# Graph-network layers on one core: mask stores issued by GpSimd, and the last x block normed by VectorE

## The chip, the core and the metric

The kernel runs on one core of a Trainium2 chip. The metric is device time in microseconds (us) of one launch, the median of several runs; lower is better. The core's engines are TensorE (PE), VectorE (DVE), ScalarE (ACT), GpSimd (POOL) and SyncE (SP). SP here only issues DMAs; ACT and POOL issue some too. Each of the three has a DMA queue of its own in the profile: q1 for SP, q10 for ACT, q0 for POOL.

## The reference, cut to what matters

`x` is 8192 x 128, `adj` is 8192 x 8192 float32 and holds ones and zeros.

```python
h = jnp.maximum(_layernorm(x), 0.0)
Wh = h @ W                                   # layer 0: attention over the graph
e = leaky_relu(Wh @ a1 + (Wh @ a2).T, 0.2)
att = softmax(where(adj > 0, e, -9e15), axis=-1)
x = x + relu(att @ Wh)
h = jnp.maximum(_layernorm(x), 0.0)
node = h @ W1                                # layer 1: K = 16 heads
hw = einsum('nc,kcf->nkf', h, W2)
y = adj @ einsum('nk,nkf->nf', node, hw) + node @ b
x = x + relu(y)
```

So `adj` (256 MB) is needed twice: as a mask in layer 0, and as a matrix in layer 1.

## The kernel before

**Setup.** The eight blocks of x (1024 rows each) are loaded, normed, turned by PE, passed through relu by ACT and multiplied by W and the two attention vectors. In `norm` (L1000 to L1007 for VectorE, L450 to L459 for GpSimd) VectorE norms four of a block's eight tiles and GpSimd the other four. `turn_x(i, g)` on PE (L812) transposes half g of block i and waits for VectorE (g = 0) or GpSimd (g = 1). `take_wh` on ACT copies the products out to `wh_mask`. The last step, i = 7, is x block 0. Extremes of the second attention vector then go through VectorE and PE to `gmm`, from which exponentials `bcol`, `qcol`, `zcol` and the row `zb` are made. Row z of all blocks is stored to HBM (`zrow_d`) and comes back block by block through `load_z` on GpSimd.

**Stage 1, the attention.** There are 8 blocks of 1024 output rows, and 8 half-turns to a block. One turn is two half-turns, p = 0 and 1, numbered n from 0 to 63. For a turn, four quarters c of `adj` (2 MB each, in four quadrants of 32 partitions; SP loads quadrants 0 and 1, ACT 2 and 3) come into `adj_sb`. They are cast to bytes `m8` (half h of each quarter for half-turn p = h; mostly by ACT, L612) and transposed in 32 x 32 squares by VectorE (`turn_squares`, L1020) into `mt[:, p]`, the mask tile of a half-turn. A quarter is loaded again once both of its casts are done. VectorE then weighs: eight `scalar_tensor_tensor` per half-turn (L1104) make `p_sb` from `zb`, `qcol` and the mask, and PE multiplies them (L901, 128 products of 128 x 129 per half-turn) into three PSUM banks. `squared` counts the squares, four to a half-turn.

**The mask store.** Layer 1 needs the same masks, so each `mt[:, p]`, 1 MB, is stored to `maskT_d` in HBM. This is done by ACT in `turn` (L712), at k = 0 of each half-turn, after waiting for the four squares of that half-turn: L723 to L728. VectorE waits for `mt_stored` before it writes the same buffer again, two half-turns later.

**The finish.** From block 1 on the rows of the block before are finished, one tile of 128 rows (number m) per half-turn, in `finish_tile` of each engine. VectorE divides, adds x (L1085, which waits for `kept`), takes statistics and norms (L1097). PE transposes (L879), multiplies with W1 (L867) and W2 (L872). ACT scales 16 heads into `prod` (L686). GpSimd first waits in `confirm` (L475 to L479) until the stores of the tile before have landed and counts `kept`. It then adds the heads up in `fold` (L485, L488), cuts the sum in two parts (L500, L502), stores it to `msg_d` (L505), and stores x1 and the bias to `keep_d` (L510). The last block's tiles are finished in stage 2.

**Stage 2.** The masks are read back from `maskT_d`, widened, and PE multiplies them with the messages (L960).

**Order on GpSimd.** After setup: wait for `z_stored`, `start_block(0)` (issues `load_z(1)`), then for each block from 1 on `start_block` and eight times `finish_tile`.

Of the kernel before, what the change touches and what calls it, by code (L numbers as in the profile page):

```python
# [35 lines left out]
EDGE = 64.0  # L36


def build(nc, x, adj, W, a1, a2, W1, W2, b, out):
# [34 lines left out]
    with ctx:  # L74
# [273 lines left out]
        def _(sp):  # L348

            sp.sem_inc(xt_in, 16 * A)  # L350
            load_x(sp, 1, (0, 1))
            for i in range(2, NB, 2):
                load_x_pair(sp, i, (0, 1))
# [78 lines left out]
        def _(pool):  # L432
# [30 lines left out]
            pool.tensor_scalar(f1rep, ones[:, :], wa[:, 0:1], None, ALU.mult).then_inc(f1rep_done, 1)  # L463
            for i in range(1, NB):
                norm(i)
# [50 lines left out]

            pool.wait_ge(z_stored, 16)

            def start_block(ib, last):
                if not last:  # L520
# [3 lines left out]
                    load_z(ib + 1)  # L524

            def finish_block(ib):
                with pool.Fori(0, IT) as jg:
                    for p in range(2):
                        u = ib * IT + jg
                        finish_tile(p, u, 2 * u + p)  # L530

            start_block(0, False)
            with pool.Fori(0, NB - 2) as before:
# [31 lines left out]
        def _(act):  # L565
            load_x(act, 1, (2, 3))
            for i in range(2, 6, 2):
                load_x_pair(act, i, (2, 3))
            act.sem_inc(node_copied, 1)
# [6 lines left out]
            load_x(act, 0, (2, 3))  # L576
            load_quadrants(act, 0, 0, 0, (2, 3))

# [36 lines left out]
            deviation(0)  # L615
            load_quadrants(act, 0, 0, 1, (2, 3))
            act.wait_ge(setup_pe, 1)
# [6 lines left out]
            for i in range(NB):  # L624
# [5 lines left out]
                if i < 2:  # L630
                    load_quadrants(act, 0, 0, 2 + i, (2, 3))
            act.wait_ge(setup_pe, 3)
            act.activation(w1T, mt_ps[1][0:K, 0:D], ACT.Copy).then_inc(setup_act, 1)
            cast(3, 0, 1, 0)
            act.activation(std[:, :], eps[:, :], ACT.Exp)
            act.wait_ge(setup_dve, 12)
# [9 lines left out]
            for c in range(A):  # L646
                if c >= 2:
                    cast(c, 1, 1, 0)
                if c < 3:
                    load_upper(1, c)  # L650
# [61 lines left out]
            def turn(i, ib, jg, finish, last):  # L712
                for p in range(2):
                    n = 2 * i + p
                    ends = ends_block(jg) and p == 1
                    sums_wait = ends and not finish
                    for k in range(C):

                        if k == 1:
                            load_upper(i + 1 + p, 3 - 2 * p)  # L720
                        if k == 3 and not sums_wait:
                            load_upper(i + 2, 2 * p)
                        if k == 0:  # L723
                            act.wait_ge(squared, A * n + A)
                            act.dma_start(maskT_d[bass.ds(2 * jg + p, 1), bass.ds(ib, 1), :, :]
                                          .rearrange("s i p w -> (s i p) w"),
                                          mt[:, p, :, :].rearrange("p c n -> p (c n)")).then_inc(mt_stored[p], 16)
                        if ends and last and k == 2:  # L728
                            load_xt(act, ib)
                        if ends and k == 3:  # L730
                            if last:
                                convert(0, True, 0)
                            copy_sums(ib)
                            if sums_wait:
                                load_upper(i + 2, 2 * p)
                        ahead = None if last else lambda: cast(2 * p + 1, 0, i + 2, 2 * A * i + 2 * p + 2)
                        if finish:
                            u = i - IT
                            finish_tile(k, p, u, 2 * u + p, 2 * jg + p, ib - 1, ahead)
                        elif k == 2 and ahead:  # L740
                            ahead()
                        if k < 2 and not last:
                            cast(2 * p, k, i + 2, A * (2 * i + k) + 2 * p + 1)
                        if k == (3 if sums_wait else 2) and not last:
                            cast(2 * p + 1, 1, i + 2, A * (2 * i + 1) + 2 * p + 2)
# [49 lines left out]
        def _(pe):  # L795
# [16 lines left out]
            def turn_x(i, g):  # L812
                pe.wait_ge(xn8_pool if g else xn8_done, i + 1)
                if i:
                    pe.wait_ge(hT_done, 2 * (i - 1) + g + 1)
                for j in range(4):
                    ins = pe.transpose(mt_ps[g][:, j * D:(j + 1) * D], xn8[:, i % 2, 4 * g + j, :], ident[:, :])
                ins.then_inc(xnT_done, 1)
# [16 lines left out]
            for i in range(NB):  # L835
# [3 lines left out]
                project(i)  # L839
                if i < NB - 1:  # L840
                    idle_run(4, h_ps)
            pe.wait_ge(f1rep_done, 1)
            for g in range(2):
                pe.matmul(hw_ps[g][:, :], f1rep, hT4[:, (NB - 1) % 2, g, :], start=True, stop=True).then_inc(f1_done, 1)

            pe.wait_ge(hT_done, 2 * NB)
            pe.wait_ge(par1_in, 32)
            pe.transpose(mt_ps[1][0:K, 0:D], wcat[:, K * D:K * D + K], ident[:, :]).then_inc(setup_pe, 1)
            pe.wait_ge(setup_dve, 4)
# [4 lines left out]
              .then_inc(setup_pe, 1)  # L854
            pe.wait_ge(setup_act, 3)
            pe.matmul(mt_ps[1][:, 2 * D:3 * D], hrep[:, :], w_sb[:, :], start=True, stop=True).then_inc(setup_pe, 1)
# [126 lines left out]
        def _(dve):  # L983
# [3 lines left out]
            def statistics(i):  # L987
                bk = block_of(i)
                dve.wait_ge(x_in[bk if bk < 2 else bk // 2 * 2], 16 * A)
                for n in range(T * i, T * (i + 1)):  # L990
# [7 lines left out]
            def norm(i):  # L998
# [3 lines left out]
                if i >= 2:  # L1002
                    dve.wait_ge(xnT_done, 2 * (i - 1))
                for t in range(HT):
                    n = T * i + t
                    ins = dve.tensor_scalar(xn8[:, i % 2, t, :], rows_of(block_of(i))[:, t, :], mv8[:, n, 0:1], rstd8[:, n:n + 1],
                                            ALU.subtract, ALU.mult)  # L1007
                ins.then_inc(xn8_done, 1)

# [15 lines left out]

            def first_cast(c, h):
                dve.wait_ge(adj_in[c], 16 * A)
                dve.tensor_scalar(m8[:, h, c, :].rearrange("p (t n) -> p t n", n=COLS), adj_halves[:, c, :, h, :],
                                  EDGE, None, ALU.mult).then_inc(adj_cast[h][c], 1)

            for c in range(3):
                first_cast(c, 0)
                first_squares(c)
                if c < 2:
                    first_cast(c, 1)
            dve.wait_ge(wh_copied, 3 * NB)
# [204 lines left out]
```

## Time and profile before

| | us |
|---|---|
| median of three runs | 1737.59 |
| lowest and highest run | 1735.99, 1738.54 |
| the profiled execution, whole | 1738.18 |
| its span (first to last instruction) | 1736.20 |
| PE busy | 1691.8 |
| DVE busy | 1312.7 |
| ACT busy | 1084.3 |
| POOL busy | 683.9 |

The span is 1.98 us shorter than the execution. Stage 1 runs from about 59 to 1215 us. In the chain of work that ended last PE has 66%, DMA 10%, POOL 9% and DVE 7%. "Idle before" in a row of the timeline is how long that engine had nothing to do before the row, with the releaser behind it. POOLq and ACTq are the engines' sequencers, which issue DMAs and count semaphores. The granted clock of TensorE is 0.99 of full speed over the span.

### The profile page before, as it was taken

The numbers are of one execution on the slowest core, as the hardware profiler recorded it, in microseconds if no ns is written. First come the engines' busy times: TensorE is split into PE (matmuls) and PEld (weight loads), VectorE is DVE, ScalarE is ACT, GpSimd is POOL, SyncE is SP. The second block draws the span as 40 slices with busy tenths as digits, with TensorE's granted clock in tenths as the row PEclk, the third lists the DMA queues.
The fourth block names the chain that finished last, engine by engine and source line by source line (L and its number), as shares of the span: only waits on it lengthen the run. The fifth ranks groups of instructions, "written<-read, shape, count | busy, mean of one in ns | idle before, by whom it ended". The sixth has DMA issues, their size and how long they took to land.

```text
span 1736.2 us, 34518 instructions
## 1 busy us (share of the span) xinstructions
PE 1691.8 (97%) x11272; PEld 1462.3 (84%) x11272; DVE 1312.7 (76%) x1746; ACT 1084.3 (62%) x1884; POOL 683.9 (39%) x562
## 2 busy tenths in 40 slices
PE   7899999999999999999999999999999999999997
PEld 5799988889888898898888888888677788888886
DVE  7798889989889898898899998997556443433534
ACT  4555676666766676766766767663565655555554
POOL 7000256556556565565564564655535100000000
PEclk9999999999999999999999999999999999999999
DMA  9999999999999999999999999968543345354430
GB/s 293 256 385 368 359 303 301 312 309 307 304 298 316 301 303 323 296 302 327 287 311 317 296 314 303 308 193 307 204 165 127 124 169 194 138 203 147 167 145 24
DMA packets 170639, 451.65 MB, mean 260 GB/s; under 512 B 13424, under 2 KB 13520, under 8 KB 152800
## 3 DMA queue, kind: packets, MB, share of 16 engines
q1 hardware_dynamic: 82272, 223.37, 41.2%
q10 hardware_dynamic: 81328, 208.20, 38.7%
q0 software_dynamic: 6992, 19.49, 3.4%
q8 instruction: 25, 0.41, 0.1%
q14 instruction: 22, 0.18, 0.0%
HBM read 363.94 MB, written 87.07 MB: 260 GB/s over the span
## 4 chain that ended last, share of the span: by engine, by line
PE 66%; DMA 10%; POOL 9%; DVE 7%; issue 5%; ACT 1%; ACTq 0%; POOLq 0%; DVEq 0%
PE ot_ps L901 29%; PE ot_ps L960 13%; PE mt_ps L960 13%; PE hw_ps L872 9%; DMA keep_d<-keep 6%; POOL prod L485 6%; DVE p_sb L1104 3%; DMA maskT_d<-mt 3%; DMA adj_sb<-in_adj_dram 1%; POOL msg L488 1%; DVE mt L1020 1%; ACT prod L686 1%; POOL p_sb L457 1%; POOL msg L500 1%; PE h_ps L867 1%
## 5 line engine op out<-in xcount | busy, mean ns | idle before, releaser
L901 PEld LDWEIGHTS ot_ps<-wh_mask,p_sb 128*128 128x128 f32 x8192 | 942.2, 192 | 75.4 <-issue 68.5
L901 PE MATMUL ot_ps<-wh_mask,p_sb 128*128 (+1 forms) x8192 | 951.4, 276 | 15.4 <-DVE p_sb L1104 15.4
L1104 DVE SCALAR_TENSOR_TENSOR p_sb<-zb,qcol,mt 128x1024 f32<-128x1024 uint8 (+1 forms) x512 | 740.2, 1461 | 22.4 <-DVE mt L1020 9.9
L485 POOL TENSOR_TENSOR prod<-prod 128x1024 f32<-128x1024 f32 (+2 forms) x192 | 395.0, 2057 | 460.3 <-ACT prod L686 362.2
L612 ACT ACTIVATE wh_mask<-adj_sb 128x2048 uint8<-128x2048 f32 x251 | 477.9, 1935 | 59.5 <-DMA adj_sb<-in_adj_dram 39.7
L1151 DVE CAST mask<-adj_sb 128x1024 fp32r<-128x1024 uint8 x272 | 203.8, 755 | 244.4 <-PE mt_ps L960 241.6
L709 ACT ACTIVATE mask<-adj_sb 128x1024 fp32r<-128x1024 uint8 x240 | 255.1, 1064 | 176.8 <-PE ot_ps L960 176.6
L686 ACT ACTIVATE prod<-hw_ps,node 128x128 f32<-128x128 f32 x1024 | 278.7, 383 | 114.3 <-PE hw_ps L872 113.3
L960 PE MATMUL mt_ps<-mask,msgs 128*128 128x512 f32 x1024 | 283.4, 399 | 3.9 <-DVE mask L1151 3.0
L960 PE MATMUL ot_ps<-mask,msgs 128*128 128x512 f32 x1024 | 275.5, 391 | 1.3 <-DVE mask L1151 0.9
L872 PE MATMUL hw_ps<-wcat,hT 128*128 128x512 f32 x512 | 240.7, 592 | 0.0
L960 PEld LDWEIGHTS mt_ps<-mask,msgs 128*128 128x128 f32 x1024 | 191.6, 188 | 53.3 <-issue 14.8
L960 PEld LDWEIGHTS ot_ps<-mask,msgs 128*128 128x128 f32 x1024 | 192.3, 188 | 44.1 <-issue 3.7
L1020 DVE STREAM_TRANSPOSE mt<-wh_mask 128x512 f32<-128x512 f32 x256 | 179.7, 702 | 20.1 <-DMA maskT_d<-mt 18.5
L872 PEld LDWEIGHTS hw_ps<-wcat,hT 128*128 128x128 f32 x512 | 88.6, 190 | 61.8 <-issue 61.2
L662 ACT ACTIVATE hT<-h_ps 128x128 f32<-128x128 f32 x64 | 17.8, 278 | 130.2 <-PE h_ps L879 129.9
L1085 DVE TENSOR_TENSOR keep<-att,xt 128x128 f32<-128x128 f32 x64 | 29.1, 454 | 84.8 <-POOLq L479 72.5
L488 POOL TENSOR_TENSOR msg<-prod 128x128 f32<-128x128 f32 x64 | 87.1, 1360 | 5.0
L676 ACT ACTIVATE node<-h_ps 128x16 f32<-128x16 f32 x64 | 11.8, 184 | 104.7 <-PE h_ps L867 104.7
L1097 DVE TENSOR_SCALAR xn<-keep,mv,rstd 128x128 f32<-128x128 f32 x64 | 60.6, 947 | 2.3
L513 POOL DMA_DIRECT2D zb<-zrow_d x7 | 3.9, 554 | 126.7 <-DVE p_sb L1104 101.0
L505 POOL DMA_DIRECT2D msg_d<-msg x56 | 31.8, 567 | 43.6 <-ACT keep L678 28.2
(129 smaller groups left out, 586.2 us busy)
## 6 DMA issues: line engine op xcount, KB each, us to landing
adj_sb<-in_adj_dram ACTq DMA_DIRECT2D x256, 512.0 KB, 12.2
adj_sb<-in_adj_dram SPq DMA_DIRECT2D x256, 512.0 KB, 11.0
maskT_d<-mt ACTq DMA_DIRECT2D x64, 1024.0 KB, 10.2
adj_sb<-maskT_d SPq DMA_DIRECT2D x32, 2048.0 KB, 7.7
keep_d<-keep POOLq DMA_DIRECT2D x64, 128.0 KB, 5.4
p_sb<-keep_d SPq DMA_DIRECT2D x4, 2048.0 KB, 11.9
msg_d<-msg POOLq DMA_DIRECT2D x56, 128.0 KB, 5.5
msgs<-msg_d SPq DMA_DIRECT2D x7, 1024.0 KB, 9.3
```

The costliest lines, as they stand in the source:

```text
L485: pool.tensor_tensor(prod[:, 0:n, :], prod[:, 0:n, :], prod[:, n:2 * n, :], ALU.add)\
L488: pool.tensor_tensor(msg32[:, :], prod[:, 0, :], prod[:, 1, :], ALU.add).then_inc(prod_read, 1)
L612: act.activation(m8[:, h, c, :].rearrange("p (t n) -> p t n", n=COLS), adj_halves[:, c, :, h, :], ACT.Copy, scale=EDGE).then_inc(adj_cast[ ...
L686: ins = act.activation(prod[:, head, :], hw_ps[g % 2][:, j * D:(j + 1) * D], ACT.Copy, scale=node[:, head:head + 1])
L709: act.activation(mask32[:, r, ib, :], masks[:, s % 4, ib, t % T // 4, :, t % 4], ACT.Copy)\
L872: pe.matmul(hw_ps[g % 2][:, :], hT[:, :], wcat[:, g * HB:(g + 1) * HB], start=True, stop=True)\
L901: ins = pe.matmul(ot_ps[h][:, (t - t0) * ROW:(t - t0 + 1) * ROW], p_sb[:, r, t * P:(t + 1) * P], rows, start=begin and t == t0, stop=end a ...
L960: ins = pe.matmul(acc_ps[2 * ib + h][:, :], msgs[:, ORDER[s] * T + t % T, c, :], mask32[:, r, ib, h * HB:(h + 1) * HB], start=t == 0 and c ...
L1020: dve.transpose(mt_squares[:, p, c, :, :, :], m8_squares[:, p, c, :, :, :]).then_inc(squared, 1)
L1097: dve.tensor_scalar(xn[:, :], x1, mv[:, 0:1], rstd[:, :], ALU.subtract, ALU.mult)\
L1104: dve.scalar_tensor_tensor(p_sb[:, r, :], zbf[:, bass.ds((ib % 2) * BLK, BLK)], qcol[:, bass.ds(tile + b_, 1)], mtb[:, p, k // 2, :, 2 * ( ...
L1151: dve.tensor_copy(mask32[:, r, ib, :], masks[:, s % 4, ib, t % T // 4, :, t % 4])\
```

## The change

GpSimd no longer norms its half of the last x block. VectorE norms both halves and counts `xn8_done` once for each. All 64 mask stores go from ACT to GpSimd, in a new `store_mask`. Eight of them (block 0) stand in a loop of their own ahead of the wait for `z_stored` and `load_z(1)`. The other 56 stand ahead of `finish_tile` in each pass of `finish_block`. Around that, x blocks 2 and 3 are loaded singly and not as a pair. VectorE casts only half 0 of quarters 0 to 2, and ACT casts half 1 of all four quarters, behind the exponentials. The load of ACT's quadrants of quarter 0 stands behind `deviation(0)`. The transpose and copy of W1 are done at x block 1 and 2 of the setup loop in another PSUM bank. The load of the Exp table is moved ahead of the last `take_wh`, and PE's idle run after the last but one block is gone.

```diff
@@ sync
-            load_x(sp, 1, (0, 1))
-            for i in range(2, NB, 2):
+            for i in range(1, 4):
+                load_x(sp, i, (0, 1))
+            for i in range(4, NB, 2):
                 load_x_pair(sp, i, (0, 1))
@@ gpsimd
-            for i in range(1, NB):
+            for i in range(1, NB - 1):
                 norm(i)
...
-            pool.wait_ge(z_stored, 16)
-
...
+            def store_mask(ib, jg, p):
+                pool.wait_ge(squared, A * (NB * ib + 2 * jg + p) + A)
+                pool.sem_inc(past_pool, 1)
+                pool.dma_start(maskT_d[bass.ds(2 * jg + p, 1), bass.ds(ib, 1), :, :].rearrange("s i p w -> (s i p) w"),
+                               mt[:, p, :, :].rearrange("p c n -> p (c n)")).then_inc(mt_stored[p], 16)
+
             def finish_block(ib):
                 with pool.Fori(0, IT) as jg:
                     for p in range(2):
                         u = ib * IT + jg
+                        store_mask(ib + 1, jg, p)
                         finish_tile(p, u, 2 * u + p)
 
+            with pool.Fori(0, IT) as jg:
+                for p in range(2):
+                    store_mask(0, jg, p)
+            pool.wait_ge(z_stored, 16)
             start_block(0, False)
@@ scalar
             deviation(0)
-            load_quadrants(act, 0, 0, 1, (2, 3))
+            for c in range(2):
+                load_quadrants(act, 0, 0, c, (2, 3))
...
-            act.wait_ge(setup_pe, 3)
-            act.activation(w1T, mt_ps[1][0:K, 0:D], ACT.Copy).then_inc(setup_act, 1)
+                if i == 2:
+                    act.wait_ge(setup_pe, 3)
+                    act.activation(w1T, hw_ps[1][0:K, 0:D], ACT.Copy).then_inc(setup_act, 1)
+                if i == NB - 2:
+                    act.activation(std[:, :], eps[:, :], ACT.Exp)
             cast(3, 0, 1, 0)
-            act.activation(std[:, :], eps[:, :], ACT.Exp)
...
             for c in range(A):
-                if c >= 2:
-                    cast(c, 1, 1, 0)
+                cast(c, 1, 1, 0)
...
-                        if k == 0:
-                            act.wait_ge(squared, A * n + A)
-                            act.dma_start(maskT_d[bass.ds(2 * jg + p, 1), bass.ds(ib, 1), :, :]
-                                          .rearrange("s i p w -> (s i p) w"),
-                                          mt[:, p, :, :].rearrange("p c n -> p (c n)")).then_inc(mt_stored[p], 16)
@@ tensor
             def turn_x(i, g):
-                pe.wait_ge(xn8_pool if g else xn8_done, i + 1)
+                if i == NB - 1:
+                    pe.wait_ge(xn8_done, i + 1 + g)
+                else:
+                    pe.wait_ge(xn8_pool if g else xn8_done, i + 1)
...
-            pe.transpose(mt_ps[1][0:K, 0:D], wcat[:, K * D:K * D + K], ident[:, :]).then_inc(setup_pe, 1)
@@ vector
-                for t in range(HT):
-                    n = T * i + t
-                    ins = dve.tensor_scalar(xn8[:, i % 2, t, :], rows_of(block_of(i))[:, t, :], mv8[:, n, 0:1], rstd8[:, n:n + 1],
-                                            ALU.subtract, ALU.mult)
-                ins.then_inc(xn8_done, 1)
+                for g in range(2 if i == NB - 1 else 1):
+                    for t in range(HT * g, HT * g + HT):
+                        n = T * i + t
+                        ins = dve.tensor_scalar(xn8[:, i % 2, t, :], rows_of(block_of(i))[:, t, :], mv8[:, n, 0:1], rstd8[:, n:n + 1],
+                                                ALU.subtract, ALU.mult)
+                    ins.then_inc(xn8_done, 1)
...
             for c in range(3):
-                first_cast(c, 0)
+                first_cast(c)
                 first_squares(c)
-                if c < 2:
-                    first_cast(c, 1)
```

## Rows read from the trace of the kernel before

**Rows 1.** The page, part 1: busy time and share of each engine.

```profile
PE 1691.8 (97%) x11272; PEld 1462.3 (84%) x11272; DVE 1312.7 (76%) x1746; ACT 1084.3 (62%) x1884; POOL 683.9 (39%) x562
```

**Rows 2.** Stretches: length, busy PE, PEld, DVE, ACT, POOL; clock, DMA share, GB/s.

```profile
70.00:183.00 113.00, 108.34 (x954) 106.85 (x952) 96.61 (x95) 57.04 (x33) 1.18 (x2) 1.00 1.05 377
...
212.00:1184.00 972.00, 964.57 (x7367) 858.56 (x7367) 870.32 (x1027) 659.94 (x1287) 554.99 (x428) 1.00 1.03 302
```

**Rows 3.** Timeline, end of setup: start, us, engine, line, operation [idle before].

```profile
38.57 1.25 DVE L1006 TENSOR_SCALAR p_sb<-xt,p_sb 128x128 f32<-128x128 f32 x4
...
38.70 6.15 POOL L457 TENSOR_SCALAR p_sb<-xt,p_sb 128x128 f32<-128x128 f32 x4
...
41.91 0.60 PE L817 MATMUL mt_ps<-ident,p_sb 128*128 128x128 f32 x4
...
43.22 22.90 SPq L326 DMA_DIRECT2D adj_sb<-in_adj_dram  x8
...
52.04 1.89 ACT L612 ACTIVATE wh_mask<-adj_sb 128x2048 uint8<-128x2048 f32 x1
...
53.95 1.28 ACT L635 ACT_TABLE_LOAD   x1
...
57.65 4.86 DVE L1104 SCALAR_TENSOR_TENSOR p_sb<-zb,qcol,mt 128x1024 f32<-128x1024 f32 x4
```

**Rows 4.** Timeline of PE in block 0; brackets show a gap.

```profile
58.98 20.88 PE L901 MATMUL ot_ps<-wh_mask,p_sb 128*128 128x129 f32 x160 [1.22 <-DVE p_sb L1104]
...
82.67 3.83 PE L901 MATMUL ot_ps<-wh_mask,p_sb 128*128 x32 [2.81 <-DVE p_sb L1104]
...
161.46 30.64 PE L901 MATMUL ot_ps<-wh_mask,p_sb 128*128 x272 [0.29 <-DVE p_sb L1104]
```

**Rows 5.** Waits, whole run: engine, for what: us, times, longest.

```profile
DVE mt L1020 <- DMA maskT_d<-mt: 18.5, 8, 6.6
...
ACT wh_mask L612 <- DMA adj_sb<-in_adj_dram: 39.7, 15, 6.3
```

**Rows 6.** Timeline of PE: the transposes of h, one to a half-turn.

```profile
191.93 0.27 PE L879 MATMUL h_ps<-ident,xn 128*128 128x128 f32 x1
...
560.57 0.27 PE L879 MATMUL h_ps<-ident,xn 128*128 128x128 f32 x1
...
578.65 0.27 PE L879 MATMUL h_ps<-ident,xn 128*128 128x128 f32 x1
...
1204.18 0.27 PE L879 MATMUL h_ps<-ident,xn 128*128 128x128 f32 x1
```

**Rows 7.** Timeline of all engines ahead of one gap.

```profile
583.23 0.54 POOL L510 DMA_DIRECT2D keep_d<-keep  x1
...
584.54 0.71 DVE L1020 STREAM_TRANSPOSE mt<-wh_mask 128x512 f32<-128x512 f32 x1
...
588.42 0.36 ACTq L725 DMA_DIRECT2D maskT_d<-mt  x1
...
589.73 0.29 DVE L1085 TENSOR_TENSOR keep<-att,xt 128x128 f32<-128x128 f32 x1 [3.13 <-POOLq L479]
```

**Rows 8.** Timelines of ACTq, POOL and DVE in block 0.

```profile
67.46 0.59 ACTq L725 DMA_DIRECT2D maskT_d<-mt  x1
...
77.98 0.64 POOL L513 DMA_DIRECT2D zb<-zrow_d  x1 [21.79 <-DMA zrow_d<-small]
...
165.41 0.71 DVE L1020 STREAM_TRANSPOSE mt<-wh_mask 128x512 f32<-128x512 f32 x1
...
179.41 5.08 DVE L1104 SCALAR_TENSOR_TENSOR p_sb<-zb,qcol,mt 128x1024 f32<-128x1024 f32 x4
```

**Rows 9.** DMA issues: KB each, median us from issue to landing.

```profile
maskT_d<-mt ACTq DMA_DIRECT2D x64, 1024.0 KB, 10.2
...
zb<-zrow_d POOLq DMA_DIRECT2D x7, 512.0 KB, 9.3
```

**Rows 10.** The keep stores from 205 to 1180 us, by tile.

```profile
DMA to landing us min/median/max: 2.0/5.4/7.8
```

More of the change, by code:

```diff
@@ L565, in _ @@
         def _(act):
-            load_x(act, 1, (2, 3))
-            for i in range(2, 6, 2):
-                load_x_pair(act, i, (2, 3))
+            for i in range(1, 4):
+                load_x(act, i, (2, 3))
+            load_x_pair(act, 4, (2, 3))
             act.sem_inc(node_copied, 1)
@@ L576, in _ @@
             load_x(act, 0, (2, 3))
-            load_quadrants(act, 0, 0, 0, (2, 3))
             act.sem_inc(out_stored, 128)
@@ L839, in _ @@
                 project(i)
-                if i < NB - 1:
+                if i == 1:
+                    pe.wait_ge(par1_in, 32)
+                    pe.transpose(hw_ps[1][0:K, 0:D], wcat[:, K * D:K * D + K], ident[:, :]).then_inc(setup_pe, 1)
+                if i < NB - 2:
                     idle_run(4, h_ps)
             pe.wait_ge(f1rep_done, 1)
+            pe.wait_ge(setup_act, 3)
             for g in range(2):
                 pe.matmul(hw_ps[g][:, :], f1rep, hT4[:, (NB - 1) % 2, g, :], start=True, stop=True).then_inc(f1_done, 1)
-            pe.wait_ge(hT_done, 2 * NB)
-            pe.wait_ge(par1_in, 32)
-            pe.transpose(mt_ps[1][0:K, 0:D], wcat[:, K * D:K * D + K], ident[:, :]).then_inc(setup_pe, 1)
             pe.wait_ge(setup_dve, 4)
@@ L854, in _ @@
               .then_inc(setup_pe, 1)
-            pe.wait_ge(setup_act, 3)
             pe.matmul(mt_ps[1][:, 2 * D:3 * D], hrep[:, :], w_sb[:, :], start=True, stop=True).then_inc(setup_pe, 1)
@@ L988, in statistics @@
                 bk = block_of(i)
-                dve.wait_ge(x_in[bk if bk < 2 else bk // 2 * 2], 16 * A)
+                dve.wait_ge(x_in[bk if bk < 4 else bk // 2 * 2], 16 * A)
                 for n in range(T * i, T * (i + 1)):
@@ L1024, in first_squares, with first_cast @@
                 turn_squares(0, c)
-            def first_cast(c, h):
+            def first_cast(c):
                 dve.wait_ge(adj_in[c], 16 * A)
-                dve.tensor_scalar(m8[:, h, c, :].rearrange("p (t n) -> p t n", n=COLS), adj_halves[:, c, :, h, :],
-                                  EDGE, None, ALU.mult).then_inc(adj_cast[h][c], 1)
+                dve.tensor_scalar(m8[:, 0, c, :].rearrange("p (t n) -> p t n", n=COLS), adj_halves[:, c, :, 0, :],
+                                  EDGE, None, ALU.mult).then_inc(adj_cast[0][c], 1)
             for c in range(3):
-                first_cast(c, 0)
+                first_cast(c)
                 first_squares(c)
-                if c < 2:
-                    first_cast(c, 1)
             dve.wait_ge(wh_copied, 3 * NB)
```

## The prediction

> **What bounds the kernel now.** I read the page first. PE is busy 97% of the span, more than any other engine [rows 1], so only idle time of PE, or of what feeds it, can be won. A table of stretches then splits the span: in the first block of stage 1 (70 to 183 us) the DMA engines are never idle and move 377 GB/s; in the rest of stage 1 (212 to 1184 us) they move 302 GB/s and PE is busy 99% [rows 2]. Where PE idles I took from its timeline.
>
> Three places matter.
>
> (1) The setup, up to the first weighted tile. The last x block is normed half by VectorE, in 1.25 us, and half by GpSimd, in 6.15 us [rows 3]. VectorE's first weighing starts at 57.65 us, and PE at 58.98 [rows 3, 4].
>
> (2) Block 0, eight half-turns without finish work. PE's timeline has seven gaps between 59 and 192 us, the first 2.81 us long and the last 0.29; with 0.28, 0.42, 0.29, 0.29 and 0.26 between them that is 4.6 us [rows 4]. VectorE waits there for mask stores to leave `mt`: 18.5 us in 8 waits, the longest, 6.6 us, just ahead of the 2.81 us gap. ScalarE waits 39.7 us in 15 waits for adj loads [rows 5]; all of both lie before 212 us.
>
> (3) Blocks 1 to 7. A half-turn without a gap is 18.08 us between two transposes of h. From 191.93 to 1204.18 us there are 55 half-turns, 1012.3 us, where 55 x 18.08 = 994.4: 17.8 us of gaps [rows 6]. The chain behind a gap is that of the keep store: GpSimd issues it at 583.23, VectorE's x1 addition waits 3.13 us and starts at 589.73 [rows 7]. So the path fold, cuts, keep store, landing, next fold takes about as long as PE's 18.08 us, and its landing is in series.
>
> **The change part by part. Setup.** VectorE norms all eight tiles: its four cost 1.25 us, eight cost 2.5, so it ends near 41.0 instead of GpSimd's 44.85 [rows 3]. PE has turned the block's first half at 42.51 [rows 3] and can go straight on to the second, 2.3 us before GpSimd's end now; ScalarE's copies follow. The Exp table load, 1.28 us, now stands ahead of the last copies and delays them by about 0.4: they end some 1.9 us earlier, near 48.5. ScalarE's cast of quarter 3 stood at 52.04 behind the copy of w1T, whose transpose was queued on PE behind the f1 products; that transpose is now early, so the cast starts right behind the last copy, at about 48.5. That is 3.5 us earlier, and the squares of quarter 3, the copy of gmm and the first weighing (57.65) follow it [rows 3]. Term: -3.4 us. Bounds: -1.9 (the copies' gain alone) and -4.5 (the table load out of the way too).
>
> VectorE also loses two casts of the other half to ScalarE. ScalarE does four instead of two, at 1.9 us each as the cast at 52.04, between the exponentials and half-turn 0, with about 1.2 us of DMA issues between them. Starting 3.4 us earlier, its last ends some 0.5 us later than now, near 65.4; VectorE wants it at about 67. This is free by 1.5 us. What it moves are the loads that these casts release: SP's loads of quarters 0 and 1 of the next turn, 2 MB, started from 43.22 on [rows 3], now start near 56. At 377 GB/s [rows 2] that is 5.6 us of transfer time given up ahead of a stretch in which the DMA engines have no pause.
>
> **Block 0.** The store of the first mask was issued by ScalarE at 67.46, behind its casts and tables [rows 8]; GpSimd can issue it as soon as it has left setup, near 53 us, while little moves. The others leave ScalarE's DMA queue, where they were ahead of and behind adj loads, and are issued when the fourth square is done. A half-turn without finish work is 128 products; 272 of them take 30.64 us [rows 4], so it is 14.4 us, and `mt` has two buffers. A store that waits behind less than now is gone before its buffer is wanted, and VectorE's waits go. Late next are the adj loads, whose casts already wait [rows 5]. Need: 5.24 million bytes to a half-turn of 14.4 us is 364 GB/s, against 377 measured [rows 2], so PE's pace can just be held. Term: -3.8 us of the 4.6. Bounds: -4.6, and +1.8 if the 5.6 us of lost prefetch come back in full where the masks gave 3.8.
>
> The Trainium skill (DMA: Bandwidth & Descriptors, section Issuing engines are not separate DMA queues) says that issuers share the same 16 engines and that spreading DMAs over issuers only saves issue time. The 377 GB/s with no idle DMA engine agree as to the sum of the bytes. By it alone the term would be between zero and the gap that one early store removes (-2.8), and the sum 1 us less.
>
> **The row of z.** `load_z(1)` waited in front of block 0 and was issued at 77.98 [rows 8]; now it stands behind all eight stores. The squares of half-turn 7 are done at 166.1 now [rows 8], 157 to 158 after the shifts above; its store and then the z row are issued, 1.5 MB on one queue. With 9.3 us as the z row's median landing [rows 9] and as much as 4 more for the store ahead of it, it is there at about 169 to 172. VectorE wants it at 179.41 [rows 8] less 8, at 171, and PE starts block 1 some 3 us behind that. Term: +0.5; bounds 0 and +4.
>
> **Blocks 1 to 7.** Now the store stands between keep store m-1 and the confirmation that the same store has landed. GpSimd waits for the fourth square, which is done at 585.24, 1.5 us behind the keep issue [rows 7], and issues for 0.54 us if it is like the keep issue. Queued behind that are `confirm`, `kept` (VectorE's x1 and ScalarE's bias copy wait for it) and the fold. The keep store lands only at about 589.6, so 3.8 us of cover are left, and the wait costs nothing. If the cover were gone, each microsecond would add one to GpSimd's path. The new store is behind the keep store in its queue, and begins some 2.6 us earlier than ScalarE's at 588.42 [rows 7], 14 us ahead of the next keep store; a mask store lands in 10.2 us [rows 9]. So neither delays the other by queue order. ScalarE loses an issue of 0.36 us [rows 7], which stands right behind the scalings that the fold waits for. At most 55 x 0.36 / 2 = 9.9 us (a path over two half-turns), at least 0, as issues run beside the engine's work. I take -2.0, nearer to zero. Bounds of the whole part: -17.8 (every gap goes) and, if the landing of keep grows, a loss with no gap to hide in.
>
> **Sum.** -3.4 - 3.8 + 0.5 - 2.0 = -8.7. The profiled execution took 1738.18 us (span 1736.20 and 1.98 around it): 1729.5. It is 0.6 above the median of the runs, so the forecast is 1729 us, 0.5% faster.
>
> **Rivals.**
> A. GpSimd's path relaxes as well. If ScalarE without the store, and adj loads without a mask in front, bring the keep landings down from 5.4 us [rows 10], most of the 17.8 us go: 1729 - 15.8 = 1713. For it: the gaps are all of that chain. Against: at keep time no mask store is in flight now either.
> B. The transfers take it back. The 2 MB that are no longer prefetched cost 5.6 us in block 0: 1729 + 5.6 = 1735. For it: ScalarE's 39.7 us of waits for adj [rows 5]. Against: 377 GB/s is a little above the need, and all four quadrants of a quarter are now under way together, not two early and two late.
> C. The slower one: the landing of the keep store, in series on GpSimd's path in blocks 1 to 7. The mask megabyte is now on the same queue, 2 us behind it, and shares the engines with it. Each 1 us more of landing costs 0.5 to 1 us a half-turn, on 55 half-turns 28 to 55 us. 0.5 us more gives +14 to +28, so 1743 to 1757. It decides from 0.16 to 0.3 us on, where it has eaten the 8.7. For it: landings go from 2.0 to 7.8 us by what is in flight [rows 10]. Against: the order in the queue.
> D. The change doesn't shorten the setup, as another input of gmm or another table load ends as late: 1729 + 3.4 = 1732.
>
> The Trainium skill (SBUF — State Buffer, section SBUF: two separate sides) warns that a DMA issued by GpSimd needs descriptors which GpSimd can't write while VectorE is in a two-port mode, and so starves. Here GpSimd's issues take 0.54 us beside a busy VectorE [rows 7]. By the rule an issue would wait out one VectorE instruction, and the cover is longer than that; it would feed rival C only.
>
> **How the numbers follow.** Forecast with its terms a few us either way (1722 to 1732.5): 0.48. A: 0.15. B: 0.15, most of it within 0.2% of before. D: 0.05. C: 0.17. 0.2% is 3.5 us, about what a measurement of this kernel can tell from no change. Faster by more: 0.48 + 0.15 + 0.05 + 0.03 of B = 0.71; same 0.12; slower 0.17. The range reaches into A and C, and leaves out the far ends of both: 1715 to 1743.
>
> **What would show it.** PE's first weighted product near 55.5; VectorE's waits for mask stores in block 0 gone; transposes of h at 183 to 184 for the first half-turn of block 1 instead of 191.93; `zb` no releaser of a wait; gaps in blocks 1 to 7 at 14 to 18 us in all; keep landings at 5.4 us. Wrong if keep lands later, if GpSimd's mask issue takes over 1 us, or if VectorE waits for adj casts in block 0.

## The result, and the profile after

The changed kernel takes 1879.89 us (median, 1877.82 to 1880.27) against 1736.79 (1735.73 to 1738.54) before: ratio 1.0822, 95% interval 1.0808 to 1.0836, so 8.2% slower. The forecast was 1729 us, and 1743 was the upper end of its range.

The page after, part 1, the chain that ended last by engine, and two rows of part 6 (KB each, median us from issue to landing):

```profile
PE 1734.0 (92%) x11268; PEld 1502.2 (80%) x11268; DVE 1272.3 (68%) x1748; ACT 1086.6 (58%) x1886; POOL 627.2 (33%) x622
...
PE 48%; DMA 20%; POOL 14%; issue 6%; DVE 5%; ACT 3%; ACTq 1%; SPq 1%; POOLq 1%; DVEq 0%
...
maskT_d<-mt POOLq DMA_DIRECT2D x64, 1024.0 KB, 8.6
...
keep_d<-keep POOLq DMA_DIRECT2D x64, 128.0 KB, 5.2
```

PE falls from 97% of the span [rows 1] to 92%, and DMA is now 20% of the chain, where it was 10%. Yet neither transfer became longer: a mask store lands in 8.6 us where it took 10.2 [rows 9], a keep store in 5.2 us (5.4 before [rows 10]). It is not the length of a transfer that grew; more transfers lie on the path.

The waits after, whole run, and the stretch of rows 2 (length, busy PE, PEld, DVE, ACT, POOL; clock, DMA share, GB/s):

```profile
DVE mt L1030 <- DMA maskT_d<-mt: 226.1, 33, 10.0
...
212.00:1184.00 972.00, 881.69 (x6425) 785.80 (x6424) 723.10 (x893) 578.84 (x1120) 437.89 (x427) 0.96 1.03 270
```

VectorE waits 226.1 us, in 33 waits, for mask stores to leave `mt`, none of them in block 0. Before it was 18.5 us, 14.9 of them in block 0 [rows 5]. In equal time PE makes 6425 products where it made 7367 [rows 2].

Where the time went is read from the transposes of h, the first and the 56th:

```profile
195.57 0.27 PE L888 MATMUL h_ps<-ident,xn 128*128 128x128 f32 x1
...
1344.93 0.27 PE L888 MATMUL h_ps<-ident,xn 128*128 128x128 f32 x1
```

Against 191.93 and 1204.18 [rows 6]: setup and block 0 +3.6 us; the 55 half-turns between the two 1149.4 instead of 1012.3, +137.1; what follows 532.97 (1877.9 - 1344.93) instead of 532.02, +1.0. The sum, 141.7, is the difference of the spans. In blocks 1 to 7 most half-turns alternate between 18.1 and 22 to 25 us.

The timeline of all engines around two of them:

```profile
600.80 0.70 DVE L1030 STREAM_TRANSPOSE mt<-wh_mask 128x512 f32<-128x512 f32 x1
...
606.39 0.71 DVE L1030 STREAM_TRANSPOSE mt<-wh_mask 128x512 f32<-128x512 f32 x1 [1.89 <-DMA maskT_d<-mt]
...
616.80 0.27 PE L888 MATMUL h_ps<-ident,xn 128*128 128x128 f32 x1
...
619.80 0.70 DVE L1030 STREAM_TRANSPOSE mt<-wh_mask 128x512 f32<-128x512 f32 x1
...
620.17 0.54 POOL L511 DMA_DIRECT2D keep_d<-keep  x1
...
621.31 0.54 POOL L528 DMA_DIRECT2D maskT_d<-mt  x1 [0.60 <-issue]
...
627.62 5.40 POOL L486 TENSOR_TENSOR prod<-prod 128x1024 f32<-128x1024 f32 x3 [5.77 <-ACT prod L697]
...
629.21 0.71 DVE L1030 STREAM_TRANSPOSE mt<-wh_mask 128x512 f32<-128x512 f32 x1 [5.72 <-DMA maskT_d<-mt]
...
636.82 0.54 POOL L511 DMA_DIRECT2D keep_d<-keep  x1
...
637.65 0.54 POOL L528 DMA_DIRECT2D maskT_d<-mt  x1 [0.29 <-issue]
...
646.92 0.71 DVE L1030 STREAM_TRANSPOSE mt<-wh_mask 128x512 f32<-128x512 f32 x1 [1.91 <-DMA maskT_d<-mt]
```

The squares at 600.80 are the fourth of a mask, those at 606.39 the first of the next mask, in the other buffer, and those at 619.80 its fourth. GpSimd stores the first mask only at 621.31, 19.8 us after its last squares are done (601.50), and the second at 637.65, 17.2 us after. Each time the keep store of the tile before stands ahead of it by about 1 us. The squares at 629.21 are the first of the third mask, in the buffer of the first: they wait for the store of 621.31 to land, and those at 646.92 for the store of 637.65.

So a cycle has closed, 40.5 us for two half-turns (606.39 to 646.92): mask store lands, VectorE squares and weighs and norms, PE transposes h and multiplies, ScalarE scales, GpSimd folds, cuts, stores keep, and only then stores the mask.

### The profile page after: what moved, and what is told of

Its sections match the earlier page's. It is cut to its first block, busy times and chain, and to the rows that moved or that the text cites. A ratio compares the mean times of both kernels' runs of the same rounds, so it can differ in the third digit from the quotient of the medians.

```text
span 1877.9 us, 34624 instructions
## 1 busy us (share of the span) xinstructions
PE 1734.0 (92%) x11268; PEld 1502.2 (80%) x11268; DVE 1272.3 (68%) x1748; ACT 1086.6 (58%) x1886; POOL 627.2 (33%) x622
## 4 chain that ended last, share of the span: by engine, by line
PE 48%; DMA 20%; POOL 14%; issue 6%; DVE 5%; ACT 3%; ACTq 1%; SPq 1%; POOLq 1%; DVEq 0%
PE ot_ps L910 17%; DMA maskT_d<-mt 14%; PE mt_ps L969 12%; PE ot_ps L969 12%; POOL prod L486 9%; DMA adj_sb<-in_adj_dram 6%; PE hw_ps L881 5%; DVE p_sb L1112 3%; ACT prod L697 2%; POOL msg L489 2%; POOL msg L501 1%; SPq L326 1%; POOL msg L503 1%; ACTq L326 1%; DMA keep_d<-keep 1%
## 5 line engine op out<-in xcount | busy, mean ns | idle before, releaser
L910 PEld LDWEIGHTS ot_ps<-wh_mask,p_sb 128*128 128x128 f32 x8192 | 980.4, 199 | 180.3 <-issue 149.2
L910 PE MATMUL ot_ps<-wh_mask,p_sb 128*128 (+1 forms) x8192 | 992.8, 282 | 117.2 <-DVE p_sb L1112 117.2
L1112 DVE SCALAR_TENSOR_TENSOR p_sb<-zb,qcol,mt 128x1024 f32<-128x1024 uint8 (+1 forms) x512 | 696.9, 1377 | 36.9 <-PE ot_ps L910 24.4
L486 POOL TENSOR_TENSOR prod<-prod 128x1024 f32<-128x1024 f32 (+2 forms) x192 | 341.9, 1780 | 629.6 <-ACT prod L697 583.0
L1030 DVE STREAM_TRANSPOSE mt<-wh_mask 128x512 f32<-128x512 f32 x256 | 180.2, 704 | 250.0 <-DMA maskT_d<-mt 226.1
L679 ACT ACTIVATE std<-mv,eps 128x1 f32<-128x1 f32 x64 | 20.3, 317 | 156.6 <-DVE mv L1099 156.6
L528 POOL DMA_DIRECT2D maskT_d<-mt x64 | 34.5, 539 | 135.1 <-DVE mt L1030 109.8
L489 POOL TENSOR_TENSOR msg<-prod 128x128 f32<-128x128 f32 x64 | 70.0, 1094 | 5.0
L1105 DVE TENSOR_SCALAR xn<-keep,mv,rstd 128x128 f32<-128x128 f32 x64 | 46.6, 727 | 2.3
```

What stands on the lines that cost most here:

```text
L486: pool.tensor_tensor(prod[:, 0:n, :], prod[:, 0:n, :], prod[:, n:2 * n, :], ALU.add)\
L489: pool.tensor_tensor(msg32[:, :], prod[:, 0, :], prod[:, 1, :], ALU.add).then_inc(prod_read, 1)
L910: ins = pe.matmul(ot_ps[h][:, (t - t0) * ROW:(t - t0 + 1) * ROW], p_sb[:, r, t * P:(t + 1) * P], rows, start=begin and t == t0, stop=end a ...
L1030: dve.transpose(mt_squares[:, p, c, :, :, :], m8_squares[:, p, c, :, :, :]).then_inc(squared, 1)
L1105: dve.tensor_scalar(xn[:, :], x1, mv[:, 0:1], rstd[:, :], ALU.subtract, ALU.mult)\
L1112: dve.scalar_tensor_tensor(p_sb[:, r, :], zbf[:, bass.ds((ib % 2) * BLK, BLK)], qcol[:, bass.ds(tile + b_, 1)], mtb[:, p, k // 2, :, 2 * ( ...
```

## The experiments

**Theory P (place).** The loss comes from where the 56 stores stand on GpSimd: behind the whole finish of a tile, a half-turn after ScalarE did it. The rivals: the loss lies in the setup and the casts; or it is GpSimd's queue and the bytes in it; or GpSimd's path grows by the issue and its wait. For each kernel the 55 half-turns are the time between the first transpose of h and the 56th, as in rows 6. Both columns come from the one profiled execution of each kernel. A ratio is to executions of before taken beside that kernel, whose medians were 1735.65 to 1736.79.

| kernel | median us | ratio to before (95%) | first h | 55 half-turns |
|---|---|---|---|---|
| before | 1736.79 | | 191.93 | 1012.3 |
| after | 1879.89 | 1.0822 (1.0808, 1.0836) | 195.57 | 1149.4 |
| e2, stores alone | 1876.03 | 1.0811 (1.0793, 1.0829) | 191.34 | 1150.4 |
| e3, setup alone | 1736.80 | 1.0007 (0.9997, 1.0018) | 193.57 | 1009.2 |
| e4, store ahead of fold | 1782.30 | 1.0275 (1.0240, 1.0309) | 192.22 | 1057.9 |
| e4c, e4 with the casts of before | 1765.04 | 1.0198 (1.0151, 1.0244) | 184.24 | 1048.1 |
| l3, ScalarE stores at k = 3 | 2036.60 | 1.1746 (1.1723, 1.1769) | 193.87 | 1307.4 |
| l2, ScalarE stores at k = 2 | 1803.31 | 1.0371 (1.0338, 1.0403) | 191.24 | 1083.2 |
| e5, next mask at the same place | 1752.33 | 1.0094 (1.0072, 1.0117) | 193.57 | 1025.5 |
| e5c, e5 with the casts of before | 1740.08 | 1.0026 (1.0007, 1.0045) | 184.38 | 1020.8 |
| e3c, e3 with the casts of before | 1729.48 | 0.9957 (0.9941, 0.9973) | 188.99 | 1012.2 |
| e6, GpSimd for block 0 alone | 1727.18 | 0.9945 (0.9927, 0.9964) | 184.62 | 1007.0 |
| h1, half of each mask | 1839.73 | 1.0607 (1.0577, 1.0637) | 185.99 | 1121.8 |

### The two halves of the change

e2 is before with only the stores moved. e3 is after with the stores put back on ScalarE:

```diff
-                        store_mask(ib + 1, jg, p)
 ...
+                        if k == 0:
+                            act.wait_ge(squared, A * n + A)
+                            act.dma_start(maskT_d[...], mt[:, p, :, :]...).then_inc(mt_stored[p], 16)
```

> The kernel before with the 64 mask stores alone moved to GpSimd, at the places of the changed kernel; setup and casts as before. Theory P (place): in blocks 1 to 7 the store of half-turn n stands on GpSimd behind the whole finish of the tile before, some 12 us after its four squares, and must land before VectorE can write that buffer again; that costs the 137 us seen in blocks 1 to 7. So 1737 + 137, less up to 5 us of mask waits in block 0: 1868 to 1876 us. Theory S (setup and casts are part of it): the loss comes in part with the moved casts and loads, and this run is faster than 1850.

> The changed kernel with all 64 mask stores back on ScalarE at k = 0; setup, casts and loads as changed. Theory P: blocks 1 to 7 as before (17 us of gaps, 2-half-turn period 36.2 us), the first weighted product near 55.5 us, and block 0 slower by the lost prefetch of 2 MB: gaps of 10 to 16 us instead of 4.6. In all 1738 to 1746. Theory S: over 1770.

e2 has the whole loss, in the same 55 half-turns (1150.4 against 1149.4 us), with the same wait. VectorE's waits from 195 to 1200 us in e2:

```profile
DVE mt L1024 <- DMA maskT_d<-mt: 194.7, 28, 9.8
```

e2 came out at 1876.03, at the upper edge of its 1868 to 1876. e3 can't be told from before; its 1736.80 lies just under its 1738 to 1746. The setup and the casts are not the cause.

### An earlier place: ahead of the fold

e4 stores the mask of the next half-turn after `confirm` and before the fold:

```diff
                 confirm(1 - p, u + 1)
+                if ahead:
+                    ahead()          # store_mask of half-turn m + 9
 ...
-                        store_mask(ib + 1, jg, p)
```

> The changed kernel, with each store of blocks 1 to 7 one place earlier on GpSimd: the store of half-turn n + 1 stands between confirm and the fold of the tile finished in half-turn n, where GpSimd waits for ScalarE's scalings anyway. Same engine, same queue, same bytes. Theory P: blocks 1 to 7 at 36.2 to 37 us for two half-turns, VectorE's waits for mask stores under 10 us, total 1738 to 1748 (block 0 as in the changed kernel). Theory Q (queue: a megabyte on GpSimd's queue is slow, or slows the keep stores, wherever it stands): still over 1800.

This missed: 1782.30 us where 1738 to 1748 was expected. GpSimd's waits and VectorE's for GpSimd, e4, 195 to 1200 us, and a store of its timeline:

```profile
POOL maskT_d L530 <- issue: 201.5, 35, 7.8
POOL maskT_d L530 <- DMA keep_d<-keep: 108.5, 16, 8.8
DVE keep L1101 <- POOLq L480: 93.7, 42, 6.9
...
802.07 0.54 POOL L530 DMA_DIRECT2D maskT_d<-mt  x1 [7.94 <-DMA keep_d<-keep]
...
802.62 6.46 POOL L486 TENSOR_TENSOR prod<-prod 128x1024 f32<-128x1024 f32 x3
```

VectorE no longer waits for mask stores at all, so lateness was cured, and 91.5 of the 137.1 us came back (1149.4 - 1057.9). But the issue now stands between the landing of keep and the fold, and at 802.07 the fold follows it at once, without a wait for ScalarE: there GpSimd's path has no cover. The 55 half-turns take 48.7 us more than in e3, which has the same setup and casts. This isn't spread evenly. In most blocks some five half-turns in eight still take 18.08 us, and the loss lies in the others. That the place of the issue makes all of it is argued from such rows; no run separates it. The prediction feared this cost for GpSimd's path, and it is seen here, not at the place of the change.

e4c is e4 with two casts given back to VectorE:

```diff
             for c in range(A):
-                cast(c, 1, 1, 0)
+                if c >= 2:
+                    cast(c, 1, 1, 0)
```

> As the run with the store ahead of the fold, and VectorE again casts half 1 of quarters 0 and 1 in setup, so that SP's loads of the next turn start near 43 us as before. Theory P with lost prefetch as the cause in block 0: gaps in block 0 fall from 15 to under 6 us, first transpose of h near 184, total 1725 to 1733, faster than before. If the prefetch isn't the cause, block 0 keeps its 15 us and the total is 1738 to 1748 as in the run beside it.

The first h comes 8.0 us earlier (184.24 against 192.22) by this alone, at 184 as expected. The total of 1725 to 1733 us was missed by over 30, for blocks 1 to 7 keep the loss of e4.

### The same place, the next mask

e5 keeps the place of the change, in the landing of keep, and only takes the mask one half-turn further on:

```diff
-                        store_mask(ib + 1, jg, p)
+                        store_mask(ib + 1, jg + p, 1 - p)
 ...
             start_block(0, False)
+            store_mask(1, 0, 0)
```

> The changed kernel with one thing altered on GpSimd: the store that stands ahead of the finish of tile m is that of half-turn m + 9 and not m + 8, so the next mask, whose fourth square is done about when the keep store is issued. Same place in the queue as the changed kernel, in the shadow of the keep store's landing. Theory P (the changed kernel stores each mask a half-turn late): no wait of VectorE for masks, blocks 1 to 7 at 36.2 to 37 us for two half-turns, total 1733 to 1750. Theory F (GpSimd's path itself, 1.6 us longer by each issue wherever it stands): 20 us a half-turn as in the run with the store ahead of the fold, total 1775 to 1790. Theory Q (queue): keep landings over 6.5 us, total over 1790.

> The run before this, and VectorE casts half 1 of quarters 0 and 1 in setup again. In the pair with the store ahead of the fold this gave 17 us, 8 of them in block 0 (first transpose of h at 184.2 instead of 192.2). Expected here: first transpose near 184, total 8 us under the run before, 1725 to 1740, which would be faster than the kernel before if theory P holds; theory F: 1765.

e5 and its twin e5c take the 55 half-turns to 1025.5 and 1020.8 us, and VectorE no longer waits for mask stores: one index brings back 123.9 of the 137.1 us. With the same engine, the same queue, the same bytes and the same place in the program, that leaves lateness as the cause. The totals, 1752.33 and 1740.08 us, lie just above their ranges (to 1750 and to 1740), and e5c isn't faster than before. A stretch of e5's timeline of GpSimd and VectorE:

```profile
795.75 0.55 POOL L511 DMA_DIRECT2D keep_d<-keep  x1 [0.24 <-issue]
796.91 0.70 DVE L1038 STREAM_TRANSPOSE mt<-wh_mask 128x512 f32<-128x512 f32 x1
...
798.09 0.53 POOL L528 DMA_DIRECT2D maskT_d<-mt  x1 [0.49 <-DVE mt L1038]
...
802.95 0.29 DVE L1101 TENSOR_TENSOR keep<-att,xt 128x128 f32<-128x128 f32 x1 [3.97 <-POOLq L480]
```

Here the squares at 796.91 are the fourth of the mask that is stored at 798.09, 0.5 us after they are done, and `confirm` comes when keep has landed. This is what the prediction described, and took for the change.

A remainder is open. e5c has 8.6 us more in the 55 half-turns than e3c (1012.2) and 13.8 more than e6 (1007.0), which have the same setup and casts and these stores on ScalarE; e5 has 16.3 more than e3. The landing of the keep stores doesn't explain it: its median from 205 to 1180 us is 5.7 us in e5c, 5.8 in e3c and 5.6 in e6. GpSimd's wait for the fourth square isn't it either: e5 has 19.7 us of it in 7 waits, but e5c only 2.0 in 4. VectorE's x1 addition waits longer for `kept`, 91.9 us against 71.9 in e3c and 73.2 in e6. What makes it wait, no run separates.

### Lateness without GpSimd

l2 and l3 are before with ScalarE's stores of blocks 1 to 7 put later in ScalarE's own order:

```diff
-                        if k == 0:
+                        if k == (0 if isinstance(ib, int) and ib == 0 else 3):     # 2 in l2
```

> The kernel before, all on ScalarE and its queue, with the mask stores of blocks 1 to 7 at k = 3 of the half-turn and not at k = 0: some 13 to 14 us later, about where GpSimd issues them in the changed kernel. Theory P: the loss comes back without GpSimd: VectorE waits over 150 us for mask stores, total 1840 to 1900. Theory Q (it is GpSimd's queue or its path): under 1760.

> As the run with k = 3, at k = 2, some 7 to 9 us later than before. Under theory P the slack is about 6 us (a store lands near 506 where its buffer is wanted at 512.5), so this is 1 to 3 us too late at first: 1745 to 1800, between the two. Theory Q: as before, 1737.

VectorE's waits for mask stores, 195 to 1200 us, in l2, then in l3:

```profile
DVE mt L1020 <- DMA maskT_d<-mt: 99.9, 35, 9.9
```

```profile
DVE mt L1020 <- DMA maskT_d<-mt: 386.9, 42, 16.6
```

The loss grows with lateness, 71 us (1083.2 - 1012.3) and 295 us (1307.4 - 1012.3), and needs neither GpSimd nor its queue. In l2 the landing is longer too, 12.8 us where before has 10.2. l2 ended 3 us above its range, and l3 went far beyond the 1840 to 1900 us that were expected. Its timeline shows why:

```profile
609.69 0.70 DVE L1020 STREAM_TRANSPOSE mt<-wh_mask 128x512 f32<-128x512 f32 x1
...
614.56 0.40 ACTq L725 DMA_DIRECT2D maskT_d<-mt  x1
...
623.16 0.71 DVE L1020 STREAM_TRANSPOSE mt<-wh_mask 128x512 f32<-128x512 f32 x1 [9.75 <-DMA maskT_d<-mt]
...
632.28 0.27 PE L879 MATMUL h_ps<-ident,xn 128*128 128x128 f32 x1
...
638.71 0.37 ACTq L725 DMA_DIRECT2D maskT_d<-mt  x1
```

The store of 614.56 frees the buffer at 623.16, PE's transpose follows at 632.28, and the next store comes at 638.71, 24.2 us after the first. It stores the mask whose fourth squares stand at 609.69, 28.3 us after they were done (610.39); in the changed kernel it was 17 to 20 us. The cycle closes within one half-turn instead of two, so every half-turn pays.

### The landing itself

h1 is after with the bytes of each mask store halved, and halved where stage 2 reads them. It leaves out half of every mask, so its result is not the reference's, and only its time is of use:

```diff
-    pool.dma_start(maskT_d[..., :, :]..., mt[:, p, :, :]...)
+    pool.dma_start(maskT_d[..., :, 0:C * BLK // 2]..., mt[:, p, 0:C // 2, :]...)
```

> The changed kernel, with only the first half of each mask stored (512 KB) and read back; the messages of the other half of the sources are multiplied with stale bytes. Same place on GpSimd's queue. If the landing of the store is in series on the path over two half-turns, 41.6 us long in the changed kernel, a landing shorter by 2 to 3.5 us takes as much off every two half-turns: 55 to 95 us less, total 1785 to 1825. If the loss is the issue on GpSimd's path and not the landing: 1875 to 1880.

Its row of part 6 and its wait, 212 to 1184 us:

```profile
maskT_d<-mt POOLq DMA_DIRECT2D x64, 512.0 KB, 7.5
...
L1030 DVE STREAM_TRANSPOSE mt<-wh_mask 128x512 f32<-128x512 f32 x188 | 132.3, 704 | 165.4 <-DMA maskT_d<-mt 165.0 <-issue 0.2
```

Blocks 1 to 7 gained 27.6 us and not the 55 to 95 expected, because the landing fell by only 1.1 us for half the bytes; the total, 1839.73, missed its 1785 to 1825. 27.6 us is 1.0 us for each of the 27.5 pairs of half-turns, about what the landing lost. That fits one mask landing in series in two half-turns, as the cycle at 606.39 says. Halved bytes also leave more of the DMA engines to the other transfers, so h1 alone doesn't prove it.

### What the rest of the change is worth

e3c is e3 with the casts of before. e6 is that, with GpSimd's loop of eight stores kept for block 0, on semaphores of their own, and ScalarE's stores from block 1 on:

```diff
+                        if k == 0 and not (isinstance(ib, int) and ib == 0):
 ...
-                        store_mask(ib + 1, jg, p)
```

> As that, with block 0's stores too on ScalarE at k = 0: what is left is the setup alone without the moved casts. The first mask waits again for ScalarE at about 65 us, which held PE for 2.8 us before: first transpose at 187 to 189, total 1730 to 1734. If moving block 0's stores is worth nothing, equal to the run beside it.

> The version that the runs point to: setup and first-block stores as changed (GpSimd, ahead of everything), blocks 1 to 7 stored by ScalarE at k = 0 as before, and VectorE's two casts of half 1 kept in setup, so that the prefetch is not lost. Block 0's stores have semaphores of their own. Expected under theory P and lost prefetch: first transpose of h at 184 as in the two runs with the old casts, blocks 1 to 7 at 1009 to 1013 us as before and in the run of the setup alone, so 1727 to 1731 us, 0.3 to 0.5% faster than before.

Both beat before, by less than 1%, and after. e6, at 1727.18 us, is 0.55% faster than before, but its interval and that of e3c overlap; that block 0's stores are better on GpSimd is not shown. What is shown is the price of the two casts that ScalarE took over: in the first h 8.0 us (e4 to e4c), 9.2 us (e5 to e5c) and 4.6 us (e3 to e3c), in the medians 17.3, 12.2 and 7.3 us. Block 0 alone, from PE's first weighted product to the first h, is shorter by 6.9, 10.1 and 5.6 us. Of the rest, 9.9 and 4.7 us lie in the 55 half-turns of e4 and e5, while e3c has 3.0 more of them than e3; nothing here explains that part.

The stretches 45 to 60 us of before, then of after:

```profile
45.00:60.00 15.00, 11.30 (x65) 7.90 (x66) 10.40 (x21) 9.43 (x18) 0.96 (x2) 0.93 0.80 166
```

```profile
45.00:60.00 15.00, 12.28 (x82) 9.06 (x82) 13.07 (x24) 11.14 (x16) 1.61 (x3) 1.00 0.35 110
```

The DMA engines are busy 35% of that time where they were busy 80%, as SP's loads wait for casts that ScalarE has not made. The pairs move the casts and the loads together, so how much is the prefetch and how much ScalarE's own time is not separated.

## Why the prediction was wrong, point by point

**Setup, -3.4: right.** PE's first weighted product was looked for near 55.5, and the timeline of after has it at 55.50, 3.48 us earlier than in rows 4. The first weighing moved with it, and SP's loads start at 55.81, later than before, as forecast (near 56):

```profile
54.17 4.87 DVE L1112 SCALAR_TENSOR_TENSOR p_sb<-zb,qcol,mt 128x1024 f32<-128x1024 f32 x4
...
55.50 6.74 PE L910 MATMUL ot_ps<-wh_mask,p_sb 128*128 128x129 f32 x58 [1.22 <-DVE p_sb L1112]
55.81 4.82 SPq L326 DMA_DIRECT2D adj_sb<-in_adj_dram  x4
```

The path was right too: ScalarE's cast of quarter 3 starts at 48.53 (forecast: about 48.5). That the number fits to a tenth is in part luck. The eight other kernels with this setup (four of them with the casts of before) have their first weighted product at 52.69 to 54.70 us, and those with the setup of before at 58.38 to 60.81. Rival D is excluded, since the setup did get shorter.

**Block 0, -3.8: the wrong sign.** From the first weighted product to the first h it took 140.07 us (195.57 - 55.50) instead of 132.95: +7.1, outside the bounds of -4.6 and +1.8. Its mechanism was half right. VectorE's waits for mask stores in block 0 did go. Late next were the adj loads, as the step said, but they weren't hidden, and that is where the step failed. Part of PE's timeline of after and, behind it, the waits of the stretch 57 to 195 us:

```profile
86.52 3.83 PE L910 MATMUL ot_ps<-wh_mask,p_sb 128*128 x32 [3.08 <-DVE p_sb L1112]
...
178.94 3.84 PE L910 MATMUL ot_ps<-wh_mask,p_sb 128*128 128x129 f32 x32 [3.32 <-DVE p_sb L1112]
...
DVE mt L1030 <- ACT wh_mask L621: 23.3, 8, 6.8
...
ACT wh_mask L621 <- DMA adj_sb<-in_adj_dram: 59.2, 16, 10.1
```

The gaps come to 15.1 us where they were 4.6, ScalarE's waits for adj to 59.2 us where they were 39.7 [rows 5], and VectorE waits for its casts. That is rival B. The stores alone were worth almost nothing: e2 takes 132.33 us from the first weighted product (59.01) to the first h, 0.6 less than before and not 3.8. Its waits from 57 to 195 us show what took the place of the mask stores:

```profile
ACT wh_mask L621 <- DMA adj_sb<-in_adj_dram: 56.6, 16, 8.7
...
DVE mt L1024 <- ACT wh_mask L621: 13.1, 5, 5.2
```

The moved casts with the later loads did the rest: e3, with them and ScalarE's stores, takes 139.85 us (53.72 to 193.57), and e3c, with the casts of before, 134.30. The step priced the lost prefetch at 5.6 us, took it as hidden in its term, and let it reach +1.8 only in its bounds; the three pairs of kernels above give 5.6 to 10.1 us in block 0.

The Trainium skill (DMA: Bandwidth & Descriptors, section Issuing engines are not separate DMA queues) says that a DMA's issuer doesn't give it engines of its own. The runs agree: with the same stores from another issuer, e2's block 0 is 0.6 us shorter. What did shorten block 0 was fewer bytes (h1, with 4 MB less to store there: 131.29 us where after has 140.07) and an earlier start of the loads (the pairs above), and the change started 2 MB later.

**The row of z, +0.5: nothing.** It was issued at 162.95 and no engine waits for it.

**Blocks 1 to 7, -2.0: this step failed, by 139 us.** It took the squares that are done at 585.24 [rows 7] for the fourth of the mask that GpSimd would store behind the keep store of 583.23. They are the first of the mask after next, in the buffer of the mask to be stored: the very write that must wait for the store. The trace of before had all that the right answer needs. These are VectorE's squares and ScalarE's store there:

```profile
563.02 0.70 DVE L1020 STREAM_TRANSPOSE mt<-wh_mask 128x512 f32<-128x512 f32 x1
...
570.20 0.36 ACTq L725 DMA_DIRECT2D maskT_d<-mt  x1
```

The mask done at 563.72 was stored at 570.20, landed some 10.2 us later [rows 9], near 580.4, and its buffer was wanted at 584.54: 4 us to spare. GpSimd, behind the keep issue of 583.23 and its 0.54 us, issues it near 583.8. With 8.6 to 10.2 us of landing the buffer is free at 592.4 to 594.0, 7.9 to 9.5 us too late. So the store that the prediction had begin 2.6 us earlier than ScalarE's begins 13.6 us later (583.8 against 570.2). The sentence on cover looked at what stands behind the new wait on GpSimd (`confirm` and the fold), found that safe, and never asked when the buffer comes free. That GpSimd's own wait costs nothing came true in the changed kernel: the fold waits for ScalarE at 627.62, not for `confirm`. But there GpSimd has time, because VectorE is late; that is no test of the forecast. e5 and e5c, where the store is the one that the prediction meant, are 16.3 and 8.6 us slower in these half-turns than their twins e3 and e3c. So -2.0 would have had the wrong sign there too.

Had this been seen, the size was not out of reach: a buffer some 8 us late is of the order of what was measured, 5.0 us for two half-turns (137.1 / 27.5). That is said with the result known, and no run tests it as a rule.

**The rivals.** None held the mechanism. C, the slower one, named this stretch and this queue, and had keep land later; keep lands in 5.2 us where it took 5.4 [rows 10]. A asked for less waiting at `confirm`; VectorE does wait less there (9.7 us where it was 72.5), for it is late itself. The -2.0 for ScalarE's lost issue can't be seen: kernels with ScalarE's stores lie between 1007.0 and 1012.3 us.

**Starved issues.** The Trainium skill (SBUF — State Buffer, section SBUF: two separate sides) has GpSimd locked out of a port that it shares with VectorE while VectorE is in a two-port mode, so that it can't write the descriptors of its DMAs. Here GpSimd's 64 mask issues took 0.53 to 0.65 us each, so the issue itself was not held, and the landings behind them were not longer than before.

## What to carry to other kernels

Where a store that frees a buffer is moved, work out first when the buffer's next writer wants it, from the last write, the issue at the new place and the landing, and only then look at what queues behind the new wait; write down for each row which index of the loop it belongs to. When such a store went to an engine whose work runs a half-turn behind, it needed its index one further on (e5), and even then the stores were no better off than on ScalarE. Casts that release loads ahead of a stretch with saturated DMA engines are not free because they fit in their engine's time: 2 MB are 5.6 us by the bandwidth, and moving their casts cost 5.6 to 10.1 us in block 0.

## What the runs showed of the hardware

**The clock.** From 212 to 1184 us the granted clock is 0.96 in after and 1.00 in before [rows 2], and 0.92 in l3, which idles most. Behind a gap of 4.56 us, PE's timeline of after:

```profile
233.03 8.28 PE L910 MATMUL ot_ps<-wh_mask,p_sb 128*128 x48 [4.56 <-DVE p_sb L1112]
```

48 products take 8.28 us where 32 take 3.83 elsewhere, so 5.7 would do: 2.5 us more, on top of the gap. For a time PE runs at the lower of its two levels, 1.2 GHz, at a granted clock of 0.50:

```profile
233.00:237.00 4.00, 3.97 (x18) 3.98 (x19) 3.67 (x7) 2.58 (x3) 2.15 (x5) 0.50 0.96 244
```

The same went the other way at the start of block 0. From 60 to 80 us, before, then after:

```profile
60.00:80.00 20.00, 19.86 (x157) 19.67 (x156) 13.49 (x14) 14.37 (x12) 0.64 (x1) 0.88 1.05 304
```

```profile
60.00:80.00 20.00, 17.60 (x158) 17.41 (x157) 16.49 (x17) 13.21 (x11) 0.54 (x1) 1.00 1.05 343
```

Before, PE's first 160 products took 20.88 us [rows 4], at a granted clock of 0.88; by the 30.64 us for 272 they would take 18.0. After has 1.00 there. The 2.9 us were not in the prediction. They hid part of what block 0 lost: gaps +10.5 and clock -2.9 make +7.6, where +7.1 was measured.

**A store of half the size.** 512 KB of a mask land in 7.5 us (h1) where 1 MB lands in 8.6 (after): half of the bytes took 1.1 us off. The same 1 MB takes 10.2 to 10.3 us from ScalarE in before and e3, but 8.7 in l3, and 10.9 from GpSimd in e4. So the landing changes with what else is under way, and the issuer alone doesn't set it.
